# Two-layer transformer with a routed expert stage: whole rows scattered into the experts' lists in place of pairs

## The chip, the cores and the metric

The kernel runs on one core of one Trainium2 chip. The metric is the device time of one execution in microseconds; smaller is better. A core has TensorE (PE, matmuls), VectorE (DVE), ScalarE (ACT), GpSimd (POOL), SyncE (SP, which here only issues transfers) and 16 transfer engines, which serve the queue filled by SP and the queue filled by POOL.

## The reference, cut to what matters

Two layers work on 8 sequences of 512 tokens with 256 features, 4096 tokens in all. The change touches the last part of the second layer, `_L1_ffn_ref`: attention with 32 heads, then a second RMS norm, a router that gives each token its 4 best of 16 experts, and the experts' outputs summed with the router's weights.

```python
h = _rms(x, ff_ln_w)                       # x after the attention; (tokens, 256)
logits = h @ wg                            # 16 experts
topv, topi = jax.lax.top_k(logits, 4)
gate = jax.nn.softmax(topv, -1)
weights = zeros.at[..., topi].set(gate)
a = silu(einsum('bsd,edh->bseh', h, w1)) * einsum('bsd,edh->bseh', h, w3)
y = einsum('bseh,ehd->bsed', a, w2)
moe = einsum('bsed,bse->bsd', y, weights)
return x + moe
```

That result is multiplied by the layer's gate (`modr`, columns 1280 to 1535) and added to the layer's input. Everything is float32.

## The kernel before

The program is a row of phases, each with its own program per engine; `run` puts a fence between them (L197), at which every engine waits for all semaphores of the phase before. `phase_m` computes modulation rows, `phase_a` (about 30 to 1700 us) is the first attention, `phase_bc` the first expert layer and the second attention, `phase_d` (2527 to 4367 us) the third attention with the router, `phase_e` (4367 us to the end) the routed experts. Order within a phase is written out by hand: each engine runs its steps in program order and waits on semaphores. `Signal` keeps the counts (`mark` names a step, `at` gives its count), `chain` waits for the engine's own earlier results, `Ring` hands out PSUM banks.

In `phase_a` POOL has nothing but 64 small scatters into `list` (L1316 to L1319), one for every third group of exponentials, numbered c = 0 to 63.

In `phase_d` a batch is one sequence and has 64 steps (N = 64) of one head pair and one block of 128 queries. In each step TensorE makes scores, DVE takes their maxima (L2378), ACT the exponentials (L2207), DVE the reciprocal sums (L2387), POOL multiplies by these (`scale`, L2440), and TensorE transposes the result five or six steps later (`turn`, L2134). Between these, `before` pieces prepare the next batch by the table `ahead` (step 39, `h`: the normed rows for the projections, in the tile `h`) and `after` pieces finish the batch before by the table `late`: steps 14 and 15 `h2`, the second norm, into the same tile `h`; 16 `HT`, its transpose, and SP's write of the rows to `hrow` in HBM (L2026); 19 to 24 the router's logits, the four best (`top`, `topi`, as numbers `topf`), and the rank of each token in its expert's list, with `tally` the running lengths; 26 `gates`, which puts token number and weight as pairs into the tile `pair`; 27 `place`, which puts 4096 x expert + rank into `pos`; and from step 29 sixteen pieces `meta`, one a step, in each of which POOL scatters 128 pairs of 8 bytes to `meta` in HBM (L2413). At its start POOL fills `meta` with dummy entries, which point to 256 rows behind the tokens, and zeroes these rows and the two sums `acc0` and `acc1` of 4352 rows (L2444 to L2452), while SP loads the stage's inputs (L2008 to L2015), for all of which TensorE waits before its first projection.

`phase_e` first computes on DVE a table of 79 tiles (L2631 to L2650): a tile is 256 places of one expert's list; the table holds its first place (`ti[:, 0, t]`) and its expert (`ti[:, 1, t]`). SP loads X, the gates (L2511) and the table's constants ahead of it. Then for each tile t SP loads the 256 pairs (L2497; up to eight tiles ahead, when the add of tile t - 8 has landed) and the expert's weights of 768 KB (L2504, when the down product of tile t - 3 is done); POOL gathers 2 x 128 rows of `hrow` by the pairs (L2539); TensorE transposes them (L2565), multiplies by w1 and w3 (L2578) and by w2 (L2587); ACT and DVE do the activation; DVE multiplies by the weights in the pairs (L2667); and POOL adds the rows to one of the two sums with two accumulating scatters (L2548). The sums take turns: tile t adds to sum t % 2 once the add of tile t - 2 has landed, so that no two transfers in flight add to the same row. POOL's order is gather(t), add(t - 4). At the end SP loads both sums (L2523), and DVE adds them, multiplies by the gate and adds X (L2680 to L2686) in eight pieces, which SP stores (L2528).

Of the kernel before, what the change touches and what calls it, by code (L numbers as in the profile page):

```python
# [97 lines left out]
def consts():  # L98
    c = {}
# [53 lines left out]
    new = np.zeros((17 * 4096, 2), np.uint32)  # L153
    new[:, 0] = 4096 + np.arange(17 * 4096) % 256
    c["meta0"] = new
# [13 lines left out]
def program(nc, D, out):  # L169
    with ExitStack() as top:  # L170
# [261 lines left out]
        def phase_a(ctx, slots):  # L432
# [70 lines left out]
            tmp = sb("tmp", [128, 256])  # L503
            pe, dve, act, c_in = sig("a_tensor"), sig("a_vector"), sig("a_scalar"), sig("a_inputs")
# [801 lines left out]
            def pool(e):  # L1306
# [14 lines left out]
            return ((tensor, vector, scalar, pool, sync),  # L1321
                    (pe, dve, act, c_in, c_s, c_kv, c_kr, c_out, c_t, c_l, c_p, pool_, *c_x, *c_mb, *c_k6, *c_q6, *c_sel, *c_max),
# [547 lines left out]
        def phase_d(ctx, tally):  # L1870
# [19 lines left out]
            h = sb("h", [128, 4, 256])  # L1890
# [12 lines left out]
            tmp = sb("tmp", [128, 256])  # L1903
            zero = sb("zero", [128, 256])
# [11 lines left out]
            pair = sb("pair", [128, 2, 16, 2], U32)  # L1916
            pe, dve, act, pool_ = sig("d_tensor"), sig("d_vector"), sig("d_scalar"), sig("d_pool")
            c_l = sig("d_norm")
            c_in, c_h, c_n, c_x, c_o = sig("d_inputs"), sig("d_rows"), sig("d_new"), sig("d_x"), sig("d_out")
# [44 lines left out]
            late.update((29 + j, ("meta", j)) for j in range(16))  # L1964
# [34 lines left out]
            def sync(e):  # L1999
# [17 lines left out]
                def after(piece, k, b):  # L2017
# [6 lines left out]
                    elif piece == "HT":  # L2024
                        e.wait_ge(dve.sem, dve.at(("h2", b)))
                        e.dma_start(D["hrow"][512 * b:512 * b + 512, :].rearrange("(i p) d -> p i d", p=128), h[:]  # L2026
                                    ).then_inc(c_h.sem, c_h.mark(("h", b), 16))
# [201 lines left out]
            def vector(e):  # L2229
# [15 lines left out]
                def rms_rows(name, b, k, w):  # L2245
# [4 lines left out]
                    for i in (2 * k, 2 * k + 1):  # L2250
                        chain(e, dve)
                        e.scalar_tensor_tensor(h[:, i, :], y[:, i, :], rs[:, 2, i:i + 1], w, ALU.mult, ALU.mult
                                               ).then_inc(dve.sem, dve.mark((name, b)))

                def before(piece, k, b):
# [33 lines left out]
                def after(piece, k, b):  # L2289
# [5 lines left out]
                    elif piece == "h2":  # L2295
                        if k == 0 and b < 7:
                            e.wait_ge(pe.sem, pe.at(("hT", b + 1)))
                        rms_rows("h2", b, k, lnw[:, 1, :])
# [40 lines left out]
                    elif piece == "gates":  # L2339
                        if b >= 2:  # L2340
                            e.wait_ge(c_p[b % 2].sem, c_p[b % 2].at(("pair", b - 2)))
# [5 lines left out]
                        e.tensor_tensor(pair[:, b % 2, :, 1].bitcast(F32).rearrange("p (i k) -> p i k", k=4), ge[:],  # L2347
                                        gz[:, 1, :].unsqueeze(2).to_broadcast([128, 4, 4]), ALU.mult
                                        ).then_inc(dve.sem, dve.tick())
                        e.tensor_copy(pair[:, b % 2, :, 0].rearrange("p (i k) -> p i k", k=4),  # L2350
                                      tok[:, 4 * b:4 * b + 4].unsqueeze(2).to_broadcast([128, 4, 4])
                                      ).then_inc(dve.sem, dve.tick())
                    elif piece == "place":
# [7 lines left out]
                                      ).then_inc(dve.sem, dve.mark(("pos", b)))  # L2361

# [45 lines left out]
            def pool(e):  # L2408
                def after(piece, j, b):
                    if piece == "meta":  # L2410
                        if j == 0:
                            e.wait_ge(dve.sem, dve.at(("pos", b)))
                        e.indirect_dma_start(D["meta"], bass.IndirectOffsetOnAxis(pos[:, b % 2, j:j + 1], 0),  # L2413
                                             pair[:, b % 2, j, :], None
# [43 lines left out]
        def phase_e(ctx, tally):  # L2458
# [32 lines left out]
            def sync(e):  # L2491
# [22 lines left out]
                for t in range(T + 3):  # L2514
                    if t < T:
                        pairs(t)
# [274 lines left out]
```

## Time and profile before

| | us |
|---|---|
| median of three timed runs | 4997.76 (4989.64 to 5001.94) |
| span of the profiled execution, first to last instruction | 4945.7 |
| profiled execution, time besides the span | not given by the page |
| PE, DVE, ACT, POOL busy | 4241.6, 3176.8, 1929.8, 1642.4 |
| mean granted TensorE clock | 0.935 |

Busy time is that of the instructions themselves; a number in brackets behind a row of the timeline is the idle time of that engine ahead of it, and what ended it. Rows of POOL marked DMA_INDIRECT are the time in which POOL writes the transfer's descriptors, not the transfer. Landing is the time from issue to the semaphore.

### The profile page before, as it was taken

What the parts mean: (1) busy time and instruction counts of PE and PEld (TensorE: products, weight loads), DVE (VectorE), ACT (ScalarE), POOL (GpSimd) and SP (SyncE); (2) the same over time, 40 slices, a digit from 0 to 9 for tenths busy, and PEclk for the clock granted to TensorE, in tenths of its full rate; (3) what the DMA queues carried; (4) which work ended last, traced back from release to release, by engine and by line L of the source; (5) the groups of instructions that cost most, each with busy time, mean ns of one, the idle gap of its engine ahead of it and who ended that gap; (6) DMA issues with size and microseconds to landing.
All of it is one profiled execution on the core that took longest, in us unless ns stands there. A gap on an engine that the chain in (4) does not pass through costs nothing.

```text
span 4945.7 us, 68678 instructions
## 1 busy us (share of the span) xinstructions
PE 4241.6 (86%) x23426; PEld 2553.3 (52%) x23426; DVE 3176.8 (64%) x7341; ACT 1929.8 (39%) x4485; POOL 1642.4 (33%) x1384
## 2 busy tenths in 40 slices
PE   3698988888888895998858999999999999949985
PEld 1444544444454443775534555555555555547774
DVE  6788788878778775557635576666757666522223
ACT  0244435344443552322214455545555555511111
POOL 1000000000000002435004464546556554648885
PEclk6799999899999997999989999999999999979998
DMA  3211221211122106773041111111111111058888
GB/s 101 25 31 30 32 44 18 40 31 31 31 32 40 18 9 179 202 186 92 15 161 39 42 44 38 43 47 35 42 39 44 38 47 39 19 153 205 209 205 225
DMA packets 332115, 358.51 MB, mean 72 GB/s; under 512 B 177326, under 2 KB 257862, under 8 KB 330902
## 3 DMA queue, kind: packets, MB, share of 16 engines
q1 hardware_dynamic: 280888, 276.81, 21.6%
q0 software_dynamic: 47984, 76.34, 7.7%
q8 instruction: 190, 3.11, 0.3%
q14 instruction: 155, 1.27, 0.1%
q10 hardware_dynamic: 2898, 0.98, 0.1%
HBM read 212.35 MB, written 81.89 MB: 59 GB/s over the span
## 4 chain that ended last, share of the span: by engine, by line
PE 60%; DVE 22%; DMA 7%; ACT 4%; issue 3%; POOL 2%; SPq 1%; ACTq 0%; DVEq 0%; POOLq 0%
PE PS L2119 7%; DVE a_mm L1265 6%; PE PS L2104 6%; PE PS L2151 6%; PE PS L2134 5%; DMA e_xg<-hrow,e_mt 5%; PE PS L2161 4%; PE PS L914 3%; PE PS L854 2%; PE PS L1611 2%; PE PS L2122 2%; PE PS L881 2%; PE PS L719 2%; PE PS L2578 2%; PE PS L892 1%
## 5 line engine op out<-in xcount | busy, mean ns | idle before, releaser
L1265 DVE TENSOR_REDUCE a_mm<-PS 128x2 f32<-128x384 f32 (+4 forms) x1152 | 673.3, 610 | 232.6 <-PE PS L858 231.1
L2440 POOL TENSOR_TENSOR d_ef<-d_ef,d_zr 128x768 f32<-128x768 f32 (+3 forms) x512 | 640.1, 1258 | 449.9 <-DVE d_zr L2387 447.5
L1019 ACT ACTIVATE a_PT<-PS 128x512 f32<-128x512 f32 x896 | 514.9, 602 | 612.9 <-PE PS L892 397.0
L2207 ACT ACTIVATE d_ef<-PS,d_nm 128x128 f32<-128x128 f32 (+3 forms) x1024 | 529.3, 523 | 358.3 <-DVE d_zr L2387 298.6
L2378 DVE TENSOR_REDUCE d_nm<-PS 128x2 f32<-128x768 f32 (+3 forms) x512 | 419.3, 819 | 341.4 <-PE PS L2122 339.9
L1318 POOL DMA_INDIRECT list<-a_tok,slots x64 | 63.1, 986 | 1551.2 <-ACT a_PT L1019 1480.5
L2119 PE MATMUL PS<-d_k,d_q 64*128 64x128 f32 (+3 forms) x2048 | 421.3, 489 | 59.1 <-ACT d_ef L2207 41.2
L854 PE MATMUL PS<-a_K,a_Q 96*128 96x192 bf16 (+4 forms) x2048 | 420.0, 284 | 52.1 <-DVE a_mm L1265 22.9
L2134 PE MATMUL PS<-ident,d_ef 128*128 128x128 f32 x2560 | 369.2, 281 | 5.0 <-POOL d_ef L2440 4.1
L854 PEld LDWEIGHTS PS<-a_K,a_Q 80*128 80x128 bf16 (+1 forms) x2048 | 180.8, 103 | 357.3 <-DVE a_mm L1265 98.4
L2218 ACT ACTIVATE d_tf<-PS 128x512 f32<-128x512 f32 x320 | 190.7, 596 | 366.4 <-PE PS L2134 365.7
L881 PE MATMUL PS<-a_Q,a_K 83*128 83x512 bf16 (+1 forms) x704 | 273.1, 403 | 58.7 <-DVE a_mm L1265 35.2
L2119 PEld LDWEIGHTS PS<-d_k,d_q 64*128 64x128 f32 x2048 | 158.0, 189 | 293.9 <-issue 157.9
L2151 PE MATMUL PS<-d_tf,d_vt 128*64 128x512 f32 x1280 | 303.7, 604 | 3.9 <-ACT d_hT L2175 1.4
L2371 DVE TENSOR_TENSOR d_t<-PS,d_rope 128x1024 f32<-128x1024 f32 x160 | 195.2, 1224 | 168.0 <-PE PS L2104 153.7
L2134 PEld LDWEIGHTS PS<-ident,d_ef 128*128 128x128 f32 x2560 | 284.6, 146 | 6.8 <-issue 5.2
L2578 PE MATMUL PS<-e_xT,e_we 128*128 128x256 f32 x1264 | 287.1, 380 | 0.0
L2548 POOL DMA_INDIRECT acc<-e_ob,e_mt x158 | 252.1, 1596 | 60.8 <-issue 44.2
L2657 DVE TENSOR_TENSOR e_hm<-e_sg,PS 128x512 f32<-128x512 f32 x79 | 54.3, 688 | 317.9 <-PE PS L2578 289.9
L914 PE MATMUL PS<-a_PT,a_v 128*32 128x512 f32 (+1 forms) x2176 | 255.3, 559 | 3.5 <-ACT a_PT L1019 3.5
L2578 PEld LDWEIGHTS PS<-e_xT,e_we 128*128 128x128 f32 x1264 | 235.0, 191 | 28.9
L1482 POOL DMA_INDIRECT bc_big<-brow,bc_ids x126 | 119.7, 950 | 380.8 <-DMA brow<-bc_hb 241.1
(347 smaller groups left out, 8104.0 us busy)
## 6 DMA issues: line engine op xcount, KB each, us to landing
e_we<-in_exp SPq DMA_DIRECT2D x79, 768.0 KB, 5.4
d_q<-d_rr SPq DMA_DIRECT2D x512, 64.0 KB, 2.0
bc_big<-in_exp SPq DMA_DIRECT2D x63, 384.0 KB, 4.3
d_k<-d_rr SPq DMA_DIRECT2D x256, 64.0 KB, 2.0
yrow<-bc_ob SPq DMA_DIRECT2D x63, 256.0 KB, 4.6
a_Q<-scr SPq DMA_DIRECT2D x384, 32.0 KB
scr<-a_qsp SPq DMA_DIRECT2D x24, 384.0 KB, 3.0
acc<-d_zero POOLq DMA_DIRECT2D x2, 4352.0 KB, 37.6
```

What stands on the lines that cost most here:

```text
L854: e.matmul(p[:, n * k:n * k + n], Q6[0:rows, 4 * hh + g, qc], K6[0:rows, y, kind, hh, 128 * i + 128 - n:128 * i + 128], start=(k == 0), st ...
L881: mm_ = e.matmul(p[:, :], K6[0:rows, y, kind, hh, 128 * kt:128 * kt + 128], Q6[0:rows, 4 * hh:4 * hh + 4, 128 * i:128 * i + 128], start=Tr ...
L914: e.matmul(o, v, w, start=first, stop=last).then_inc(pe.sem, pe.mark(("pv", n)))
L1019: e.activation(PT[:, 4 * (n % 2) + q4, :], RS.of(("exp", n, q4))[:, :], ACT.Exp, scale=S0).then_inc(act.sem, act.mark(("exp", n, q4)))
L1265: e.tensor_reduce(mm[:, i % 2, kind, c:c + len(gs)], RP.of(("top", b, u, kind, gs[0]))[:, 0:len(gs) * n].rearrange("p (g k) -> p g k", g=l ...
L2119: e.matmul(p[:, r, 0:nk], q[rows, a % 2, hh, f, 128 * i:128 * i + 128], kd[rows, hp // 2, 2 * (hp % 2) + hh, 0:nk], start=True, stop=False)
L2134: e.transpose(p[:, 256 * f + 128 * r:256 * f + 128 * r + 128], ef[:, (2 * g + f) % 7, r, 128 * j:128 * j + 128], ident[:]).then_inc(pe.sem ...
L2151: e.matmul(p[64 * hh:64 * hh + 64, :], vt[:, b % 2, j, 64 * kv:64 * kv + 64], tf[:, place[2 * J + hh, j] % 12, :], start=(j == 0), stop=(j ...
L2207: e.activation(ef[:, n % 7, r, 0:nk], S.of(("exp", n))[:, r, 0:nk], ACT.Exp, bias=nm[:, n % 7, r:r + 1], accum_out=zz[:, n % 7, r:r + 1]). ...
L2378: e.tensor_reduce(nm[:, n % 7, :], S.of(("exp", n))[:, :, 0:128 * i + 128], AX, ALU.max, negate=True).then_inc(dve.sem, dve.mark(("max", n)))
L2440: e.tensor_tensor(ef[:, n % 7, :, 0:nk], ef[:, n % 7, :, 0:nk], zr[:, n % 7, :].unsqueeze(2).to_broadcast([128, 2, nk]), ALU.mult).then_in ...
L2578: e.matmul(p[:, 256 * m:256 * m + 256], we[:, t % 3, c0:c0 + 128], xT[:, t % 2, k, :], start=(k == 0), stop=(k == 1)).then_inc(pe.sem, pe. ...
```

## The change

Whole rows are scattered, not pairs. The tile `h` gets 9 more columns: the token number, the four weights, and the numbers of the four experts. POOL scatters each row of 265 numbers (1060 bytes) four times, to its place in each of its four experts' lists `xrow` in HBM, two scatters a step from step 28 in eight steps. The next use of the tile `h` (step 39, `h` of batch b + 2; for the last batch step 14) waits for these. The write to `hrow` is gone. The lists' first 256 rows and the sum are initialised by two transfers which POOL issues in `phase_a`, after its scatter c = 8; POOL's initial writes in `phase_d` are gone. The table is computed on DVE in `phase_d`, after the last batch's `place`, beside its scatters. A list's last tile is moved back so that it ends with the list, and rows which the tile before has already handled get the weight 0. `phase_e` loads a tile's 256 rows with one transfer from SP, takes the weight of its expert from the row's nine columns on DVE (`gates`), and adds into one sum; a tile's add waits until the add of the tile before has landed. X and the gates are loaded in eight parts during the tiles 8, 16, ... 64. The end has half of the sum's loads and two DVE operations per part in place of three.

```diff
@@ phase_a, pool
                     e.indirect_dma_start(D["list"], ...)
+                    if c == 8:
+                        e.dma_start(D["xrow"].rearrange("(e r) c -> e r c", r=4096)[:, 0:256, :],
+                                    D["row0"].unsqueeze(0).to_broadcast([17, 256, 265])).then_inc(c_n.sem, c_n.tick(16))
+                        e.dma_start(D["acc"], D["zero0"].to_broadcast([4352, 256])).then_inc(c_n.sem, c_n.tick(16))
@@ phase_d
-            late.update((29 + j, ("meta", j)) for j in range(16))
+            late.update((28 + j, ("meta", j)) for j in range(8))
@@ vector
                             if b >= 2:
                                 e.wait_ge(pe.sem, pe.at(("HT", b - 2)))
-                                e.wait_ge(c_h.sem, c_h.at(("h", b - 2)))
+                                e.wait_ge(c_p[b % 2].sem, c_p[b % 2].at(("row", b - 2)))
...
-                        e.tensor_tensor(pair[:, b % 2, :, 1]..., ge[:], gz[:, 1, :]..., ALU.mult)
-                        e.tensor_copy(pair[:, b % 2, :, 0]..., tok[:, 4 * b:4 * b + 4]...)
+                        e.tensor_tensor(h[:, :, 257:261], ge[:], gz[:, 1, :]..., ALU.mult)
+                        e.tensor_copy(h[:, :, 256:257].bitcast(U32), tok[:, 4 * b:4 * b + 4].unsqueeze(2))
+                        e.tensor_copy(h[:, :, 261:265], topf[:])
...
+                    elif piece == "meta" and k == 0 and b == 7:
+                        table()
@@ pool
-                        e.indirect_dma_start(D["meta"], bass.IndirectOffsetOnAxis(pos[:, b % 2, j:j + 1], 0),
-                                             pair[:, b % 2, j, :], None)
+                        for m in (2 * j, 2 * j + 1):
+                            e.indirect_dma_start(D["xrow"], bass.IndirectOffsetOnAxis(pos[:, b % 2, m:m + 1], 0),
+                                                 h[:, m // 4, :], None)
...
-                e.dma_start(D["meta"], D["meta0"])
-                e.dma_start(D["hrow"][4096:4352, :]..., zero[:]...)
-                for i in range(2):
-                    e.dma_start(D[f"acc{i}"]..., zero[:]...)
-                e.wait_ge(c_n.sem, c_n.at("new"))
@@ phase_e, sync
+                def rows(t):
+                    if t >= 4:
+                        e.wait_ge(pe.sem, pe.at(("xT", t - 4)))
+                        e.wait_ge(dve.sem, dve.at(("gates", t - 4)))
+                    row = e.value_load(ti[0:1, 0, t:t + 1], min_val=0, max_val=17 * 4096 - 256)
+                    e.dma_start(xg[:, t % 4, :, :].rearrange("p a c -> p (a c)"),
+                                D["xrow"][bass.ds(row, 256), :].rearrange("(p a) c -> p (a c)", a=2)
+                                ).then_inc(c_g[t % 4].sem, c_g[t % 4].mark(("rows", t), 16))
...
+                rows(0)
+                weights(0)
+                e.dma_start(place[:], D["place"])
+                for t in range(1, T + 1):
+                    if t < T:
+                        rows(t)
+                    if t >= 2:
+                        weights(t - 1)
+                    if t >= 8 and t % 8 == 0 and t < 72:
+                        later(t // 8 - 1)
@@ pool
-                for t in range(T + 4):
-                    if t < T:
-                        gather(t)
-                    if t >= 4:
-                        add(t - 4)
+                for t in range(T):
+                    e.wait_ge(dve.sem, dve.at(("out", t)))
+                    if t:
+                        e.wait_ge(c_a[(t - 1) % 2].sem, c_a[(t - 1) % 2].at(("add", t - 1)))
                     for a in range(2):
+                        e.indirect_dma_start(D["acc"], bass.IndirectOffsetOnAxis(to[:, t % 8, a:a + 1], 0),
+                                             ob[:, t % 4, a, :], None, compute_op=ALU.add
                                              ).then_inc(c_a[t % 2].sem, c_a[t % 2].mark(("add", t), 16))
@@ vector
+                def gates(t):
+                    if t >= 8:
+                        e.wait_ge(c_a[t % 2].sem, c_a[t % 2].at(("add", t - 8)))
+                    e.wait_ge(c_g[t % 4].sem, c_g[t % 4].at(("rows", t)))
+                    e.tensor_copy(to[:, t % 8, :].unsqueeze(2), xg[:, t % 4, :, 256:257].bitcast(U32))
+                    e.scalar_tensor_tensor(wt[:, t % 4, :, :], xg[:, t % 4, :, 261:265], tt[:, 0, t:t + 1],
+                                           xg[:, t % 4, :, 257:261], ALU.is_equal, ALU.mult)
+                    e.tensor_reduce(wr[:, t % 8, :], wt[:, t % 4, :, :], AX, ALU.add)
+                    e.scalar_tensor_tensor(wr[:, t % 8, :], place[:], tt[:, 1, t:t + 1], wr[:, t % 8, :], ALU.is_ge, ALU.mult)
...
                     if t < T:
                         gate(t)
+                    if t + 1 < T:
+                        gates(t + 1)
                     if t:
                         out(t - 1)
...
-                    e.tensor_tensor(ac[:, b, 0, :, :], ac[:, b, 0, :, :], ac[:, b, 1, :, :], ALU.add)
```

`table()` is the old table with one more product and sum over 80 x 16 elements and eight small operations; `later(b)` loads one eighth of X and one row of the gates.

## Rows read from the trace of the kernel before

**Rows 1.** Stage table: busy us per engine, clock, DMA share, GB/s.
```profile
core 0: us, PE busy (x) PEld busy (x) DVE busy (x) ACT busy (x) POOL busy (x), PEclk, DMA share, GB/s
4410.00:4902.00 492.00, 444.53 (x2153) 375.78 (x2151) 121.30 (x233) 90.75 (x152) 395.80 (x305) 1.00 0.85 203
4902.00:4945.70 43.70, 0.00 (x0) 0.00 (x0) 28.77 (x24) 0.00 (x0) 2.70 (x2) 0.51 0.90 297
```
**Rows 2.** Timeline of two adds and SP's pair load in the expert loop.
```profile
4595.37 1.62 POOL L2548 DMA_INDIRECT acc<-e_ob,e_mt  x1 [0.30 <-issue]
...
4597.30 1.56 POOL L2548 DMA_INDIRECT acc<-e_ob,e_mt  x1 [0.31 <-issue]
...
4601.86 0.34 SPq L2497 DMA_DIRECT2D e_mt<-meta  x1
```
**Rows 3.** POOL's indirect transfers by line: ns min/median/max, first and last start.
```profile
L2548 POOL DMA_INDIRECT acc<-e_ob,e_mt x158: 1554/1578/1638, 4410.0 to 4903.4; - x158
...
L2539 POOL DMA_INDIRECT e_xg<-hrow,e_mt x158: 942/972/1017, 4388.3 to 4881.8; - x158
...
L2413 POOL DMA_INDIRECT meta<-d_pair,d_pos x128: 954/1001/1068, 2913.8 to 4365.4; - x128
```
**Rows 4.** Chain of the expert loop: start, us, what.
```profile
4512.24 1.63 POOL acc L2548
4514.18 6.14 DMA acc<-e_ob,e_mt
...
4779.66 3.46 PE PS L2578 x16
...
4785.28 3.46 PE PS L2578 x16
```
**Rows 5.** Timeline from the last scatters to the first weight matmul.
```profile
4346.10 0.99 POOL L2413 DMA_INDIRECT meta<-d_pair,d_pos  x1 [29.51 <-DVE d_pos L2360]
...
4367.54 0.34 SPq L2507 DMA_DIRECT2D e_tab<-in_tiles  x1
...
4368.88 12.03 SPq L2511 DMA_DIRECT2D e_GB<-modr  x8
4370.37 0.18 DVE L2631 TENSOR_TENSOR e_cnt<-tally,e_tab 128x16 f32<-128x16 f32 x1 [24.54 <-DMA e_lte<-in_lte]
...
4379.05 0.20 DVE L2650 TENSOR_SCALAR e_ti<-e_tf 128x80 int32<-128x80 f32 x1
4381.72 3.66 SPq L2497 DMA_DIRECT2D e_mt<-meta  x4
...
4398.36 4.78 PE L2578 MATMUL PS<-e_xT,e_we 128*128 128x256 f32 x16
```
**Rows 6.** Timeline: SP's loads of the sums behind the last adds.
```profile
4907.14 17.64 SPq L2523 DMA_DIRECT2D e_ac<-acc  x16
```
**Rows 7.** Transfers from 2528 to 2570: all, and SP's queue.
```profile
DMA packets 4474, 16.40 MB, mean 391 GB/s; under 512 B 1040, under 2 KB 1552, under 8 KB 4074
...
q1 hardware_dynamic: 2400, 7.61, 47.3%
```
**Rows 8.** Timeline: the third attention's first projection and its operand.
```profile
2549.95 0.60 ACT L2175 ACTIVATE d_hT<-PS 128x512 f32<-128x512 f32 x1 [0.26 <-PE PS L2057]
...
2567.02 5.74 PE L2104 MATMUL PS<-d_hT,d_wk 128*128 128x512 f32 x8 [17.11 <-DMA d_tok<-in_tok]
```
**Rows 9.** Timeline of POOL in the first attention: the ninth list scatter.
```profile
404.03 0.96 POOL L1318 DMA_INDIRECT list<-a_tok,slots  x1 [13.22 <-ACT a_PT L1019]
```
**Rows 10.** Stage table of the 48 us behind it.
```profile
404.00:452.00 48.00, 39.44 (x283) 23.32 (x282) 41.88 (x129) 22.57 (x40) 1.91 (x2) 0.99 0.23 43
```
**Rows 11.** Timeline of a batch's scatters in the third attention, POOL and DVE.
```profile
2911.74 1.89 POOL L2440 TENSOR_TENSOR d_ef<-d_ef,d_zr 128x1024 f32<-128x1024 f32 x1 [1.73 <-DVE d_zr L2387]
...
2931.49 0.99 POOL L2413 DMA_INDIRECT meta<-d_pair,d_pos  x1 [0.16 <-issue]
...
2945.91 1.01 DVE L2252 SCALAR_TENSOR_TENSOR d_h<-d_y,rs,d_lnw 128x256 f32<-128x256 f32 x2
```
**Rows 12.** Page, issues: KB each, us to landing.
```profile
e_we<-in_exp SPq DMA_DIRECT2D x79, 768.0 KB, 5.4
```

More of the change, by code:

```diff
@@ L2023, in after @@
                         e.dma_start(xb[:], xout[:, 4 * b:4 * b + 4, :]).then_inc(c_x.sem, c_x.mark(("x2", b), 16))
[L2024 to L2027, printed above, removed]
+                        if b == 7:
+                            e.wait_ge(pe.sem, pe.at(("v", 7, 1, 1)))
+                            e.dma_start(tab, D["tiles"]).then_inc(c_b.sem, c_b.mark("table", 16))
+                            e.dma_start(lte, D["lte"]).then_inc(c_b.sem, c_b.mark("table", 16))
                     elif piece == "lg":
@@ L2361, in after, with reduced @@
                                       ).then_inc(dve.sem, dve.mark(("pos", b)))
+                    elif piece == "meta" and k == 0 and b == 7:
+                        table()
+                def reduced(out, a, b, op):
+                    n = out.shape[1]
+                    chain(e, dve)
+                    e.tensor_tensor(cmp[:, 0:n, :], a, b, op).then_inc(dve.sem, dve.tick())
+                    chain(e, dve)
+                    e.tensor_reduce(out, cmp[:, 0:n, :], AX, ALU.add).then_inc(dve.sem, dve.tick())
@@ L2481, in phase_e @@
             c_out = sig("e_out")
-            c_m = [sig(f"e_pairs{i}") for i in range(8)]
             c_w = [sig(f"e_weights{i}") for i in range(3)]
@@ L2505, in weights, with later @@
                                 ).then_inc(c_w[t % 3].sem, c_w[t % 3].mark(("weights", t), 16))
-                e.dma_start(tab[:], D["tiles"]).then_inc(c_in.sem, c_in.tick(16))
-                e.dma_start(lte[:], D["lte"]).then_inc(c_in.sem, c_in.mark("all", 16))
-                e.dma_start(Xs[:], xout).then_inc(c_x.sem, c_x.mark("x", 16))
-                for b in range(8):
+                def later(b):
+                    e.dma_start(Xs[:, 4 * b:4 * b + 4, :], xout[:, 4 * b:4 * b + 4, :]
+                                ).then_inc(c_x.sem, c_x.mark("x", 16))
                     e.dma_start(GB[:, b, :], D["modr"][b:b + 1, 1, 1280:1536].to_broadcast([128, 256])
                                 ).then_inc(c_gb.sem, c_gb.mark("all", 16))
-                e.wait_ge(dve.sem, dve.at("table"))
-                for t in range(T + 3):
+                rows(0)
+                weights(0)
+                e.dma_start(place[:], D["place"]).then_inc(c_in.sem, c_in.mark("all", 16))
+                for t in range(1, T + 1):
                     if t < T:
-                        pairs(t)
-                    if t >= 3:
-                        weights(t - 3)
+                        rows(t)
[3 more added lines that the diff above has]
+                        later(t // 8 - 1)
                 for i in range(2):
@@ L2646, in vector @@
-                e.tensor_scalar(tf[:, 2, :], tf[:, 0, :], 4096.0, None, ALU.mult).then_inc(dve.sem, dve.tick())
-                chain(e, dve)
-                e.scalar_tensor_tensor(ti[:, 0, :], tf[:, 1, :], 256.0, tf[:, 2, :], ALU.mult, ALU.add
-                                       ).then_inc(dve.sem, dve.tick())
-                e.tensor_scalar(ti[:, 1, :], tf[:, 0, :], 15.0, None, ALU.min).then_inc(dve.sem, dve.mark("table"))
+                    e.scalar_tensor_tensor(wr[:, t % 8, :], place[:], tt[:, 1, t:t + 1], wr[:, t % 8, :], ALU.is_ge,
+                                           ALU.mult).then_inc(dve.sem, dve.mark(("weight", t)))
@@ L2696, in program @@
         tally = sbt(top, "tally", [128, 16])
-        run(phase_d, tally)
-        run(phase_e, tally)
+        ti = sbt(top, "ti", [128, 2, 80], I32)
+        tt = sbt(top, "tt", [128, 2, 80])
+        run(phase_d, tally, ti, tt)
+        run(phase_e, ti, tt)
         for e in engines:
```

177 lines of the change are left out of this document (83 added, 94 removed).

## The prediction

> **What bounds the kernel now.** I read the stage table first, then the issue and line rows of the expert stage, then its chain and timeline. The page gives the profiled execution as a span, 4945.7 us, and no second time; the median of the three timed runs is 4997.76 us, so 52.1 us lie around the span. I make the sum on the span and add 52.1.
>
> In the stage table [rows 1] TensorE is near full only in the middle stages. From 4410 to 4902 (79 expert tiles) POOL is busy 395.8 of 492 us in 305 issues, and each issue has a 0.30 us gap before it [rows 2]: 395.8 + 305 x 0.30 = 487.3, so POOL is never free. That stage is bound by POOL's issuing: two gathers of 0.97 and two adds of 1.58 [rows 3], four gaps, 6.3 a tile. The adds begin at 4410.0 and the last of the 158 at 4903.4 [rows 3]; less one in-tile step of 1.93 [rows 2] that is (4903.4 - 4411.9)/78 = 6.30 us a tile. TensorE needs less: where its rows of the chain stand back to back, matmul block to matmul block is 4779.66 to 4785.28, 5.62 us [rows 4]. The granted clock is 1.00 there, the 2.4 GHz level, so TensorE has nothing more to give.
>
> **The expert loop: what takes the place of the gathers.** Both gathers and the pair load leave; SP loads 256 contiguous rows instead. POOL keeps two adds: 1.62 + 0.30 + 1.56 = 3.48 us. But there is now one sum, and every tile's adds wait until the tile before has landed (before: the tile before that one, which had two periods). So a period is issue plus landing plus wake-up. The landing has no row of its own; SP shows it. SP's pair load of 4601.86 waits for an add; the add before it was issued from 4595.37 and its second half ends at 4597.30 + 1.56 = 4598.86 [rows 2]: 3.0 us. Of this SP's own register work is about 0.76 (four such loads take 3.66 us, so 1.1 each, of which 0.34 is the issue [rows 5]). Landing plus wake-up: 2.24. The last adds give 4903.4 + 1.56 to SP's 4907.14: 2.1 to 2.2 [rows 3, 6]. A period is then 3.48 + 2.2 = 5.7, plus 0.1 for POOL's wake-up: 5.8.
> That is the undisturbed case. The disturbed one has a row: an add begun at 4512.24 is followed in the chain by 6.14 us of transfer from 4514.18, to 4520.32, 8.1 us after its start [rows 4]. Before, a second accumulator covered that; now it is paid. How often depends on load. The queues' engines are busy 0.85 of 6.30 us, 5.36 us a tile [rows 1]. The change swaps gathered for plain rows (about even) and spreads the loads of X and of the gates, once 5.2 MB at the stage's start, over the loop: at the tail's 297 GB/s with share 0.90 [rows 1] some 16 us, 0.2 a tile. So 5.56 of 5.8 us would be busy, 0.96: some adds must meet the weights' 768 KB. I take 6.1, one slow landing (8.1 + 0.3 against 5.8) in eight; ends 5.75 and 7.2 (half slow and the load on top). Loop: 78 x (6.10 - 6.30) = -16 us, between -43 and +70. A register load, two waits and a DMA stay on SP as before; DVE gets four small operations a tile, nearest the table's 0.18 [rows 5], under 0.8 us of a period in which DVE is busy 121 of 492 us [rows 1]. The first of them waits for the rows of tile t+1, and the output of tile t-1 is queued behind it; SP has issued those rows two tiles before TensorE turns them (it stops at the weights, which wait for the down product four tiles back), some 11 us against a landing of under 6, so this wait costs nothing, and 6 us and more if SP falls back.
>
> The Trainium skill (DMA: Bandwidth & Descriptors, Anatomy of one DMA) says a software-issued DMA costs about 2.0 us fixed, mostly the write's receipt, heaviest in HBM. It speaks against this edit, since a second sum hid that receipt. By it the 128 KB half lands 2.0 + 0.3 us after its issue, 5.8 a tile and -39 us for the loop; the undisturbed rows agree, the disturbed ones do not.
>
> **Start of the attention stage.** POOL's initial writes (two sums, pair table, dummy rows: by their shapes 9.7 MB) go. In 2528 to 2570 the engines move 16.40 MB at 391 GB/s [rows 7], while TensorE waits 17.11 us for the inputs until 2567.02; its other operand is there at 2549.95 + 0.60 [rows 8]. SP's queue has 7.61 MB of it [rows 7]; alone at that rate it takes 19.5 us, to about 2548, so the operand ends last. Gain 16.4 at most, 12 if SP's own issuing of the last inputs stays slow; I take 15.5. What is late next is that operand (DVE's norms).
> These writes, now 9.1 MB, are issued in the first attention behind the ninth list scatter, at 404.03 [rows 9]. There DMA share is 0.23, TensorE and DVE busy 39 and 42 of 48 us [rows 10]. By the rate above they land in 23 to 40 us, and SP's small loads meet them. Nobody waits for them but the stage's end, 1290 us on. Loads are early by a tile; cost 2 us, between 0 and 15. The list scatters behind them are also only awaited at the end.
>
> **Scatters of whole rows.** 128 issues stay 128. A pair scatter takes 1.00 us, a gather of 1 KB rows 0.97, an accumulating issue 1.58 [rows 3]; the width did not matter between the first two, so I take 1.00 for 1060-byte rows, ends 0.95 and 1.6. They are now two a step in eight steps. For the first such batch POOL begins with the scaling of 2911.74, and the seventh scatter stands at 2931.49 [rows 11]. Nine more by then at 1.17 are 10.5 us, of which its gaps absorb 2 or 3: the last is issued near 2940 and lands some 3 us on, as the adds do, near 2943. DVE's next use of the tile, which now waits for that, is at 2945.91. The three us cover it; behind that wait on DVE stand the maxima that every exponential needs, so uncovered it would cost. POOL's scalings come up to 5 us late, within the five steps until TensorE transposes them. I take +1, ends 0 and +47 (rival below). The row write on SP and its wait go, at nothing: no chain piece held them.
> The last batch still has 16 issues from 4346.10; the last starts at 4365.4 [rows 3, 5], and SP proceeded at 4367.54. A 135 KB landing is longer than 1 KB's: +1.2.
>
> **Start of the expert stage.** The table took 4370.37 to 4379.25 on DVE [rows 5]. Now it runs from 4346 beside the scatters, with two 1.49 us operations and a few small more: 13 us, 8 us of cover. Uncovered it would cost 13. SP's eight gate loads (12.03 us), X, and the gathers' wait for pairs go from the head. Before: 4367.5 to the first weight matmul 4398.36, 30.9 us [rows 5]. After, from the same point: register load 0.8; rows(0); weights(0) issued at 1.9, landing 5.4 later [rows 12], 7.3; rows(1) behind it, about 8; transposes 1.2: 9.3. Gain 21.6, less the 1.2 above: 20.4 (ends 15 and 23).
>
> **Tail.** Before, 12.6 MB of loads and stores and 24 DVE operations, 28.77 us [rows 1]; without the second sum 8.4 MB and 16 operations, 19.2. Gain by DVE 9.6; by bytes 4.2 MB at the stage's 297/0.90 = 330 GB/s, 12.7. The smaller decides, with the pair of first loads now one: I take 10, ends 8 and 13.
>
> **Sum.** -16 - 15.5 + 2 + 1 - 20.4 - 10 = -58.9; span 4886.8, time **4939**.
>
> **Rivals.**
> 1. *TensorE becomes the bound*: every add lands undisturbed. For it: two landings of 2.2. Against: engines 0.96 busy. Period 5.75: 78 x 0.35 = 27 less, 4912. Chance 0.2.
> 2. *The landing of the single sum takes the place of the gathers, the other side*: adds and the weights' transfer share the engines in most tiles. For it: the 8.1 us row. Against: only two adds are queued at a time now, and SP's loads wait for TensorE, which follows the adds, so the two may fall apart. At 7.2 a tile, 78 x 1.1 = 86 more, 5025, slower. It decides from 6.1 + 58.9/78 = 6.85. Chance 0.14. The Trainium skill (DMA: Bandwidth & Descriptors, Queues, rings and completion order) says that an engine alternates between queues packet by packet; that would be this mechanism.
> 3. *A 1060-byte scatter costs an accumulating issue's 1.58*: 16 x 0.58 = 9.3 us a batch; DVE's wait uncovered by 6 in six batches, 37, and 9.3 in the last: +46, 4985. Against: width was free from 8 bytes to 1 KB. Chance 0.11.
> 4. *The engines are simply full*: unaligned rows cost more than gathers, period 6.5: +31, 4970. Chance 0.1.
> The forecast, period 5.9 to 6.4, 4920 to 4965: 0.45.
>
> **How the numbers follow.** About 0.3% (15 us) is what a measurement of this kernel can tell. Faster by more: 0.45 + 0.2 + 0.08 + 0.04 = 0.77 (most of 4, part of 3); within: 0.1; slower: 0.13. Leaving out rival 2 and a little at both ends gives 4900 to 4998.
>
> **What would show it.** Period of the adds 6.1; POOL's idle time before them given to the add's own transfer, not to "issue"; first weight matmul 9 to 10 us after SP's first load; first attention matmul near 2551; 34 us from the last tile's first add to the end; scatters of 1.0 us. Wrong if the adds' period is over 6.85, or if DVE waits for scatters in the attention.

## The result, and the profile after

The changed kernel takes 5163.59 us (5156.55 to 5168.56, four runs), the kernel before 4997.91 beside it: ratio 1.0333, 95% interval 1.0319 to 1.0347. Forecast were 4939 and a range of 4900 to 4998. The change makes the kernel slower by 3.3%.

Two sizes must be kept apart first. In the profile of after the time is 5168.56 and the span 5166.8, so only 1.8 us lie around a span. The 52.1 us that the prediction put there go with the chip: the kernel before took 4998 us in the runs beside this one and in one later set of runs, 4949, 4956 and 4950 in the three others. Its profile (4945.7) has the time of the second kind of chip, the profile of after that of the first. (Each chip served for one set of runs, so what is called the chip's here could also be the occasion's.) The table therefore sets the changed kernel's second profile (run `e7_changed_again`, on a chip of the second kind) against before; each column is a distance between first or last rows of the traces.

| stretch | before | changed (e7) | difference | forecast |
|---|---|---|---|---|
| start to last list scatter | 1691.1 | 1834.9 | +143.8 | +2 |
| the middle stage (first experts, second attention), to the third attention's first transpose | 856.9 | 857.5 | +0.6 | 0 |
| to the first projection | 19.0 | 2.7 | -16.3 | -15.5 |
| to the last scatter of rows or pairs | 1798.4 | 1807.4 | +9.0 | +1 |
| to the first add | 44.6 | 24.2 | -20.4 | -20.4 |
| 78 periods of the adds (from one tile's first add to the next one's) | 491.5 | 556.5 | +65.0 | -16 |
| tail | 44.2 | 32.5 | -11.7 | -10 |
| span | 4945.7 | 5115.7 | +170.0 | -58.9 |

Two rows went wrong, the first attention and the expert loop; together they are 223 us off. All rows that follow are of the first profile of after, if nothing else is said. The first attention behind the ninth list scatter, by stretches (columns as in [rows 1]):

```profile
404.00:452.00 48.00, 21.75 (x119) 12.40 (x116) 19.38 (x43) 8.69 (x16) 5.04 (x4) 0.68 0.78 84
452.00:500.00 48.00, 26.24 (x164) 15.31 (x164) 27.14 (x93) 14.34 (x24) 0.99 (x1) 0.71 0.43 64
500.00:550.00 50.00, 0.00 (x0) 0.00 (x0) 0.00 (x0) 0.00 (x0) 0.00 (x0) 0.50 0.06 27
550.00:600.00 50.00, 3.96 (x19) 1.21 (x19) 0.00 (x0) 0.60 (x1) 0.00 (x0) 0.53 0.13 41
```

The first row answers to [rows 10], where TensorE was busy 39.44 us. In the third row no engine does anything for 50 us, and the transfer engines are busy 0.06 of the time: one sixteenth. Bandwidth is not what is short; one of the sixteen is at work. Who waits is shown by SP's queue and by the waits (us in total, times, longest):

```profile
463.22 129.39 SPq L671 DMA_DIRECT2D a_Q<-scr  x11
```
```profile
PE PS L856 <- DMA a_Q<-a_selT: 98.9, 1, 98.9
```

SP's eleven small loads take 129 us to issue, and TensorE stands 98.9 us in one wait for the load before them. Behind both is one of the two initial writes (KB, us to landing):

```profile
xrow<-in_row POOLq DMA_DIRECT2D x1, 4505.0 KB, 58.4
acc<-in_zero POOLq DMA_DIRECT2D x1, 4352.0 KB, 186.2
```

The two count on one semaphore, so the landings may be exchanged. The records of single packets tell them apart: from 407.3 to 580.5 there are 85 packets of 54,272 bytes, 2.0 us each (the first 3.4), none beside another. 85 x 54,272 bytes are the 17 x 256 dummy rows.

The third attention and the expert stage (min/median/max ns, first and last start), answering to [rows 3]; the rows of the kernel's first projection and weight matmul, to [rows 8] and [rows 5]:

```profile
L2467 POOL DMA_INDIRECT xrow<-d_h,d_pos x128: 956/991/1481, 3095.4 to 4561.3; - x128
...
L2581 POOL DMA_INDIRECT acc<-e_ob,e_to x158: 1550/1557/1616, 4585.5 to 5135.9; - x158
```
```profile
2752.04 5.88 PE L2113 MATMUL PS<-d_hT,d_wk 128*128 128x512 f32 x8 [1.20 <-DMA d_tok<-in_tok]
...
4573.46 4.76 PE L2605 MATMUL PS<-e_xT,e_we 128*128 128x256 f32 x16
```

A scatter of 1060-byte rows costs POOL 0.99 us as one of 8 bytes did. The wait before the first projection is 1.20 us, not 17.11, and the first weight matmul stands 12.2 us behind the last scatter. The adds have (5135.9 - 1.86 - 4585.5)/78 = 7.03 us a tile, before 6.30. The loop's and the tail's row of the stage table:

```profile
4585.50:5134.00 548.50, 460.75 (x2151) 384.12 (x2149) 163.88 (x537) 90.74 (x152) 242.91 (x156) 0.95 0.78 193
5134.00:5166.80 32.80, 0.00 (x0) 0.00 (x0) 18.98 (x16) 0.00 (x0) 3.11 (x2) 0.50 0.85 264
```

POOL, 395.8 of 492 us before, is now busy 242.9 of 548.5: it is no longer full, and the loop is slower all the same. The chain of waits says why. An undisturbed period and a slow one (start, us, what):

```profile
4700.89 3.73 DMA acc<-e_ob,e_to
...
4705.35 1.56 POOL acc L2581
4706.90 0.30 issue
4707.21 3.82 DMA acc<-e_ob,e_to
...
4711.76 1.56 POOL acc L2581
```
```profile
4803.36 5.96 DMA acc<-e_ob,e_to
...
4810.23 0.55 issue
4810.78 1.56 POOL acc L2581
```

Undisturbed: 1.86 from the first half's issue to the second's, 3.73 to 3.82 until that has landed, and 0.74 until POOL begins the next add: 6.3 to 6.4. The outputs between the landing and the add belong to a later tile: DVE's four buffers are full, since POOL is some four tiles behind. POOL does not wait for them: in the first seven periods, where these outputs start 2.7 to 17 us behind the landing, POOL begins 0.73 us after it as well. In the slow period the same landing takes 5.96. Slow periods are the smaller part: of the 78, 51 are under 6.6 us and 15 over 7.6, these 9.2 in the mean.

Last, a mark of the first kind of chip, in the chain of the middle stage; two of five such pieces:

```profile
2413.11 7.04 another core or an unknown queue
...
2420.93 10.43 another core or an unknown queue
```

The five make 33.7 us. The profiles of e7 and of before have none.

### The profile page after: what moved, and what is told of

The parts are those of the page before. It is cut to its first block, busy times and chain, and to the rows that moved or that the text cites. A ratio compares the mean times of both kernels' runs of the same rounds, so it can differ in the third digit from the quotient of the medians.

```text
span 5166.8 us, 68882 instructions
## 1 busy us (share of the span) xinstructions
PE 4278.3 (83%) x23426; PEld 2569.6 (50%) x23426; DVE 3225.2 (62%) x7665; ACT 1929.1 (37%) x4485; POOL 1478.2 (29%) x1223
## 4 chain that ended last, share of the span: by engine, by line
PE 54%; DVE 23%; DMA 8%; SPq 4%; issue 4%; ACT 4%; POOL 3%; another core or an unknown queue 1%; ACTq 0%; DVEq 0%; POOLq 0%
PE PS L2128 6%; PE PS L2113 6%; DMA acc<-e_ob,e_to 6%; DVE a_mm L1267 5%; PE PS L2160 5%; PE PS L2143 5%; PE PS L2170 3%; PE PS L916 3%; SPq L671 3%; PE PS L856 2%; POOL acc L2581 2%; PE PS L1617 2%; PE PS L2131 2%; PE PS L883 2%; PE PS L721 2%
## 5 line engine op out<-in xcount | busy, mean ns | idle before, releaser
L2581 POOL DMA_INDIRECT acc<-e_ob,e_to x158 | 246.0, 1557 | 329.2 <-DVE e_ob L2681 273.9
L2681 DVE TENSOR_SCALAR e_ob<-PS,e_wr 128x256 f32<-128x256 f32 x158 | 69.2, 480 | 315.6 <-DMA acc<-e_ob,e_to 299.3
L2480 POOL TENSOR_TENSOR d_rr<-d_t 128x512 f32<-128x512 f32 x80 | 101.6, 1270 | 560.4 <-DVE d_t L2424 445.6
```

## The experiments

All ratios are to the kernel before on the same chip, with the 95% interval.

**e1_rows_spread.** One transfer engine against bytes.

```diff
-  e.dma_start(D["xrow"].rearrange("(e r) c -> e r c", r=4096)[:, 0:256, :],
-              D["row0"].unsqueeze(0).to_broadcast([17, 256, 265]))
+  e.dma_start(D["xrow"].rearrange("(e r) c -> r e c", r=4096)[0:256, :, :],
+              D["row0"].unsqueeze(1).to_broadcast([256, 17, 265]))
```

> The changed kernel with one edit: the DMA that writes the 17 x 256 dummy rows runs over rows first and lists second (256 x 17 x 1060 bytes instead of 17 runs of 271 KB); bytes, place and number of DMAs stay. Theory (one transfer engine): the trace of the changed kernel has this DMA as 85 packets of 54,272 bytes, one behind the other at 2.01 us, from 407.3 to 580.5, and the small loads of the first attention wait behind them; that is the 150 us by which the first attention is longer. Then this kernel wins nearly all of it: the last list scatter near 1695 (before 1691, changed 1841), the time 5163.6 - 145 = about 5018, and the wait of TensorE from 500 to 590 gone. Rival (bytes, or the zero fill of the sum in 4 KB packets): 9.1 MB are still written at this place, so 80 us and more of the 150 stay, time over 5090. The expert loop stays at 7.0 us a tile under both.

Measured 5017.03 us, ratio 1.0148 (1.0126 to 1.0169). The time meets the 5018 only because this chip is 50 us faster: the ratio fell by 0.0185, some 92 us. The last list scatter is at 1745.1, not 1695: 90 to 96 us come back, 54 stay. Order of the dimensions alone is worth 90 us; but the rival had a part of the truth. The trace has the rest (stage table of e1):

```profile
450.00:500.00 50.00, 8.60 (x45) 3.64 (x43) 9.25 (x28) 5.65 (x8) 0.99 (x1) 0.58 0.95 71
```

All sixteen engines are busy, 0.95, at 71 GB/s: something else is slow. By the packet records it is the zero fill: its 1088 packets of 4 KB take 949 ns each (median), those of the fill of the kernel before 164 ns. The latter reads a tile of zeroes in SBUF, the former one 1 KB row of DRAM again and again. That both ends lie in DRAM does not explain it: the dummy rows' 1088 packets of 4,240 bytes, DRAM to DRAM too but from 256 different rows, take 316 ns in the same run.

**e2_two_sums.** On e1, two sums, one zero fill more, and a tail that reads and adds both.

```diff
-  if t: e.wait_ge(c_a[(t - 1) % 2].sem, c_a[(t - 1) % 2].at(("add", t - 1)))
+  if t >= 2: e.wait_ge(c_a[t % 2].sem, c_a[t % 2].at(("add", t - 2)))
-  e.indirect_dma_start(D["acc"], ...)
+  e.indirect_dma_start(D[f"acc{t % 2}"], ...)
```

> The kernel of the run before it (dummy rows spread) with two sums again: tile t adds into sum t mod 2 and waits for tile t - 2, both sums are zeroed in the first attention, and the tail reads and adds both. Theory (the single sum's landing bounds the loop: issue start 1.86 after issue start, 1.56 of issue, 2.2 to land, 0.7 for POOL to go on, 6.3 undisturbed and 7 to 9 where the landing is slow): the adds' period falls from 7.03 to TensorE's 5.6 to 5.9 us a tile, 78 x 1.2 = -94, the tail is 10 longer: 84 under the run before it, near 4935. Rival (the engines' load by whole rows and weights, 5.5 us a tile of packet time, and DVE's order bound the loop): the period stays over 6.6 and the time over 4990.

Measured 5011.99, ratio 1.0131 (1.0110 to 1.0151). The period came as expected, the total did not: the second fill from the DRAM row put the last list scatter at 1818.3, 73 us later, and ate the gain.

```profile
L2584 POOL DMA_INDIRECT acc<-e_ob,e_to x158: 1556/1562/1613, 4506.9 to 4969.4; - x158
```

(4969.4 - 1.86 - 4506.9)/78 = 5.91 us a tile, more than half of the periods 5.62, TensorE's own. With two sums the loop is fast, so the single sum is what makes it slow. Whole rows and DVE's four small operations are in this run too.

**e3_before_one_sum.** The kernel before, all tiles into `acc0`, waiting for tile t - 1; one fill and one half of the tail's work less.

> The kernel before with one sum alone: every tile adds into the same sum and waits for the tile before; one zero fill, one half of the tail's loads and additions less. Theory (the landing chain is the bound): POOL's two gathers (2.5 us with gaps) fit in the 2.9 us in which it waits for the landing, so the period is the chain's 6.3 to 7.1, not 6.3 as before: loop 0 to +60, tail -10, the attention's start -10: time between 4980 and 5050, POOL's idle time before the first add of a pair given to the add's transfer or to an output that waits for it. Rival (whole rows and not the single sum make the loop slow): period 6.3 to 6.4, POOL still full, time 4975 to 4985.

Measured 5037.49, ratio 1.0189 (1.0166 to 1.0211), within the expected time, but the period is 7.67, longer than expected. POOL in that loop:

```profile
4703.35 1.56 POOL L2548 DMA_INDIRECT acc<-e_ob,e_mt  x1 [0.30 <-PE PS L2578]
4705.22 1.01 POOL L2539 DMA_INDIRECT e_xg<-hrow,e_mt  x1 [0.30 <-issue]
4706.53 0.97 POOL L2539 DMA_INDIRECT e_xg<-hrow,e_mt  x1 [0.30 <-issue]
4709.12 1.63 POOL L2548 DMA_INDIRECT acc<-e_ob,e_mt  x1 [1.61 <-DVE e_ob L2667]
```

The gathers do fit into the wait, but the next add begins 5.77 us after the second half's issue, not 4.5. The landing is what is later: 5.0 us in the median, in the changed kernel 3.8. That the gathers' transfers, issued in between on the same queue, cause this is likely, but not shown apart. One sum alone costs 78 x 1.37 = 107 us there; the changed kernel, with one sum and no gathers, stands at 7.03 to 7.13.

**e4_half_weights.** On e1; SP returns for odd t, and tile t uses the weights of tile t - t % 2.

> The kernel of the first run (dummy rows spread, one sum) with the weights loaded for every second tile only; the odd tiles compute with the weights of the tile before. It leaves out 39 of 79 loads of 768 KB. Theory (a slow landing is an add whose packets meet the weights' transfer): landings of over 4.5 us get rare, the adds' period falls from 7.03 to 6.3 to 6.45, the chain's own length, and no lower. Rival 1 (the landing is slow by itself, for instance by the adds' own reads and writes): period stays at 6.9 to 7.1. Rival 2 (TensorE or the load of the engines is the bound): period under 6.0.

Measured 5005.49 us in one run; period 6.83. None of the three: with half the loads gone the period is 0.16 under e1's 6.99, of the 0.6 that lie over the undisturbed one. Four profiles with the same loop (after, e7, e1, e5) have 7.03, 7.13, 6.99 and 7.13, so 0.16 is hardly more than their spread.

**e5_zero_tile.** On e1, the single sum zeroed from SBUF.

```diff
-  e.dma_start(D["acc"], D["zero0"].to_broadcast([4352, 256]))
+  e.dma_start(D["acc"].rearrange("(i p) d -> p i d", p=128),
+              z0[:].unsqueeze(1).to_broadcast([128, 34, 256]))
```

> The changed kernel with spread dummy rows and, new, the sum zeroed from a tile of zeroes in SBUF (128 partitions, as the kernel before did it in its last attention) instead of from one 1 KB row of DRAM. With spread rows alone the first attention was still 54 us longer than before, and the 1088 packets of 4 KB took 949 ns each there, against 164 ns in the attention stage of the kernel before. Theory (a DRAM row that every packet reads is a slow source, 16 engines in the same place): the packets take about 170 ns, the fill 12 us instead of 65, the last list scatter stands 5 to 15 us behind before's 1691, and the time is 5017 - 43 = about 4975. Rival (small loads suffer from any 4.4 MB put at this place, whatever its source): less than 15 us come back, time over 5000.

Measured 4979.56, ratio 1.0056 (1.0039 to 1.0072). The packets take 164 ns, the last list scatter is at 1697.4. In the stretch that answers to the row of e1 above TensorE works, and the engines have room:

```profile
450.00:500.00 50.00, 39.83 (x199) 19.65 (x197) 42.46 (x100) 15.40 (x27) 1.57 (x2) 0.86 0.17 45
```

With the source, the order in which the fill writes its rows changed too, so the two are not shown apart. The 143.8 us of the first attention are therefore 90 for the dummy rows' form, 48 for the zeroes' source (with its order) and 6 that are left. In the seven traces with both mended the last list scatter starts between 1695.2 and 1705.5, so the 6 are not well resolved.

**e6_zero_tile_two_sums.** e5 with e2's two sums, both zeroed from SBUF.

> Spread rows, both sums zeroed from the SBUF tile, two sums in the expert loop. Theory: the two-sum loop at 5.9 us a tile and the cheap start of the first attention add up: 5012 - (127 - 20) = about 4905, 40 us under the kernel before on this chip (4946 by its profiled span). Rival (the first attention keeps most of its loss): over 4950.

Measured 4900.57, ratio 0.9897 (0.9881 to 0.9914): faster than before by 1%. Period 5.89.

**e8_pieces_two_sums**, and **e8_again**. On e6, the writes in 17 x 3 pieces.

```diff
-  if c == 8:     # all initial writes at once
+  if 8 <= c < 25:
+      k = c - 8  # 256 dummy rows of list k, rows 256k to 256k + 255 of both sums
```

> As the run before it (two sums, SBUF zeroes), but the initial writes cut into 17 x 3 pieces of 256 and 265 KB, three behind each list scatter from the ninth to the twenty-fifth. Theory (what costs is that small loads queue behind megabytes on every transfer engine): a piece is gone in about 2 us, so no load waits long, and the last list scatter falls to within 5 us of before's 1691; time 5 to 15 under the run before it. Rival (the bytes cost in any form, or POOL's 51 issues of about 1 us delay the list scatters' chain): the same time or more.

> The kernel with cut initial writes and two sums once more, as the partner of the next run on the same chip. Expected: the same ratio to before, 0.988 within 0.002.

Measured 4893.26, ratio 0.9876 (0.9859 to 0.9892), and again 4894.99, 0.9884 (0.9864 to 0.9904). Against e6 that is inside the intervals, and the last list scatter (1705.5, 1696.9; e6 1699.9) shows no gain: with a good form and source it hardly matters whether the writes go at once or in pieces. The repeated run came as expected.

**e7_changed_again.** The changed kernel, unedited, on this chip.

> The changed kernel, nothing edited, on this chip. In its own profile the middle stage (first experts and second attention) was about 50 us longer than before, with stretches between two TensorE instructions that name no releaser; the kernel before was also 52 us slower in its timed runs there (4998) than in its profile (4946). Theory (that belongs to the chip it ran on, and to both kernels): here the middle stage takes before's 857 us, the time is about 5165 - 52 = 5113, and the ratio to before stays 1.033. Rival (it is the change's own, the instruction stream): the stage stays 50 us long and the ratio is 1.043.

Measured 5118.02, ratio 1.0335 (1.0317 to 1.0352); middle stage 857.5. The 50 us go with the chip, in both kernels; run e11 met such a chip again (before 4998.01, its own middle stage 10 + 43 us longer).

**e9_last_scatters_apart.** On e8.

```diff
-  for m in (2 * j, 2 * j + 1):
+  for m in ((j,) if b == 6 else (2 * j, 2 * j + 1) if j < 8 else ()):
```

> The kernel of the run before it, with the 16 row scatters of the seventh batch spread over 16 steps of the last batch's attention, one a step, instead of two a step over eight. Theory (in the last batch no projections of a next one fill TensorE, and POOL's scalings come late behind two scatters a step: 1.9 + 2 x 1.29 = 4.5 us of POOL for a step of 3.4; the trace has TensorE waiting 2.6 us for a scaling at that place, and the stage from the first projection to the last scatter is 1807 instead of before's 1798): 3 to 6 us come back, the last batch's product of gates and rows starts 152 to 154 us after the one before it instead of 157. Rival (the 8 us are the lower clock of TensorE at the end and longer small operations of DVE): no change within 2 us.

Measured 4888.69, ratio 0.9876 (0.9858 to 0.9895), beside e8_again's 0.9884: the times do not resolve it. The two traces differ as expected: from first projection to last scatter 1801.4 instead of 1806.7, and between the last two batches' transposes of rows 152.8 instead of 157.3 (before 152.4). The wait it removes, in e7:

```profile
4366.87 1.79 PE L2143 MATMUL PS<-ident,d_ef 128*128 128x128 f32 x8 [2.59 <-POOL d_ef L2494]
```

This is the lowest time of the study, 61 us under before.

**e10_no_weights.** On e5, SP's `weights` returns for t >= 3, and tile t uses the weights of tile t % 3.

> The changed kernel with spread rows, SBUF zeroes and one sum, and the weights loaded for the first three tiles only; all other tiles compute with these. It leaves out 76 of 79 loads of 768 KB. With half of the loads the period fell only from 6.99 to 6.83. Theory (the slow landings, 7 to 10 us a period, are adds whose second half is queued behind a 768 KB load that SP issued between the two halves; with half the loads the others met more often): the period falls to the chain's own 6.4 to 6.5, with slow ones left only where X and the gates are loaded, every eighth tile. Rival (the adds are slow by themselves or by the row loads): it stays over 6.7.

Measured 4957.31 in one run. Period 6.88: 0.25 less than e5's, but over the 6.7 from which the rival was to be right. The weights are a part, not the cause.

**e11_rows_only.** On e10, `later(b)` for all b ahead of `rows(0)`, so that in the loop SP loads rows alone.

> The kernel of the run before (one sum, weights loaded for three tiles only, the rest of the tiles with these) and the loads of X and of the gates all at the head of the expert stage: in the loop SP loads nothing but the rows, 265 KB a tile. Theory (each load that SP puts between an add's issue and its landing makes it late; the last eight tiles of the run before, with no load left, take 6.2 to 6.4): the periods of 8 to 9.5 us at every eighth tile go, the mean falls from 6.88 to 6.7, and what stays over 6.25 is the row loads'. Rival (every eighth tile is slow by its data, for instance by its tokens): they stay. The head of the stage takes about 15 us longer under both.

Measured 5015.78 in one run, on a chip where before took 4998.01. Period 6.73, and no period over 7.61 is left, where e10 had five of 8.2 to 9.4. The three rows of adds (e5, e10, e11, in this order):

```profile
L2586 POOL DMA_INDIRECT acc<-e_ob,e_to x158: 1550/1557/1612, 4386.0 to 4944.1; - x158
```
```profile
L2586 POOL DMA_INDIRECT acc<-e_ob,e_to x158: 1551/1558/1615, 4386.3 to 4924.5; - x158
```
```profile
L2586 POOL DMA_INDIRECT acc<-e_ob,e_to x158: 1551/1557/1612, 4456.4 to 4983.1; - x158
```

7.13, 6.88, 6.73. The last eight periods of e11, when SP has nothing more to load, are 6.17 to 6.49, in the mean 6.30: the chain by itself. From e5's 7.13 the mean falls by 0.25 without the weights, by 0.15 more without X and the gates, and 0.43 are left over 6.30 in e11. These are steps in this order, not the shares of the three in e5, and the first two are near the spread of 0.14. The single periods show it:

| | under 6.6 us | over 7.6 us | median |
|---|---|---|---|
| after | 51 | 15 | 6.42 |
| e5 | 48 | 19 | 6.52 |
| e10 | 19 | 5 | 6.72 |
| e11 | 23 | 1 (7.61) | 6.73 |

Without the weights the long periods go, and the usual one gets longer: SP now issues the rows elsewhere, in most of e11's periods 1.85 us after the add's start, with its second half, where after has them some 5.0 us behind it. What the row loads cost in the changed kernel itself no run shows. What is shown is that the long periods come with the weights and with X and the gates.

What a late landing looks like is seen packet by packet in the slow period of after. The packets that start in each microsecond:

```
us        adds (1 KB)   rows (2120 B)   weights (6 KB)
4804      90            24               1
4805      62             1               0
4806      81             0              22
4807       1             0              47
4808       2            27              44
4809       0            79              14
```

SP issues the weights at 4805.12, between the issue of the add's second half (4803.36) and its landing. 253 of the add's 256 packets have started by 4806.9. The last three start at 4807.19, 4808.35 and 4808.68, among the weights' packets, and the landing is reported at 4809.32. Three late packets of 256 make the landing 2.1 us longer, and POOL's wake-up behind it is 1.46 here. But a load in that place does not always do this. In the undisturbed period above, where the add started at 4705.35 and landed in time, SP issued its weights just as late:

```profile
4708.96 0.34 SPq L2546 DMA_DIRECT2D e_we<-in_exp  x1
```

In 70 of after's 78 periods the weights are issued between the second half and its landing; 44 of these are under 6.6 us and 15 over 7.6. Of the other eight none is over 7.6. So every slow landing there had a load beside it, most landings with one were not slow, and what decides which adds are hit is open.

## Why the prediction was wrong

**First attention, +2 (0 to 15) against +144: the step that failed most.** It priced 9.1 MB "by the rate above", 391 GB/s of [rows 7], the rate of loads and of fills from SBUF, of other shapes. It did not hold: the dummy rows ran on one engine (27 GB/s), and the zeroes came from a single DRAM row (4 KB in 949 ns in e1). In place of 23 to 40 us the dummy rows alone took 173. The sentence that nobody waits for the writes but the stage's end was true and beside the point, since SP's small loads share the engines; that they "are early by a tile" was no cover against one engine taken for 173 us. What was left once form and source were mended, 6 us, lies in the range that was given. The Trainium skill (DMA: Bandwidth & Descriptors, Why a DMA increments its semaphore by 16 and not by 1) says that a transfer uses the largest number of engines up to 16 that divides the slowest dimension (other than 1) of both sides, which for 17 is one and for 256 and 4352 sixteen. For some copies issued by GpSimd it names an exception, which this one did not show. The rule could have been read against the diff before the run, and the trace agrees: 85 packets, none beside another, and a landing after 31.7 us once 256 stood first (e1).

**Expert loop, 6.10 against 7.03 to 7.13: mis-sized in two terms.** The mechanism was named: issue plus landing plus wake-up, lengthened by slow landings. The chain by itself was set at 5.8 and is 6.30 to 6.4. Issue (3.42 for 3.48) and landing (2.2 for 2.2) held; POOL's wake-up was put at 0.1 and is 0.74. That term is 50 us. The value had no row behind it, and the trace of before had one that spoke against it. POOL was never free in the loop, but ahead of it it waited for the pairs to land:

```profile
4381.72 5.77 DMA e_mt<-meta
...
4387.55 0.73 issue
4388.28 0.99 POOL e_xg L2539
```

Its first gather starts 0.79 us after that landing at 4387.49. The disturbances were put at 0.3 a tile, one period in eight at 8.4 us; they are 0.7 to 0.8, in after 15 of 78 periods, one in five, at 9.2. Rival 2 (the single sum's landing, the other side) named the direction, and its deciding period of 6.85 was passed, but only in part by its own mechanism: adds and weights meet in time in most tiles (70 of 78), yet most periods stay undisturbed (51 of 78), and the wake-up makes up the rest. It was given 0.14, on the argument that adds and loads "may fall apart"; SP's loads are released by TensorE, which follows the adds, and in these 70 periods that puts them beside each other instead.

**The third attention, +1 against +9.** The scatter's price (1.00) was right, rival 3 fell (0.99), and DVE's wait for the scatters stayed covered: batch follows batch every 218.8 us (e7), before every 218.0. POOL's late scalings were taken as harmless everywhere; in the last batch, with no projections of a next one to fill TensorE, they cost 5 (e9 against e8_again, one trace each). The other 4 were not tried; 0.8 us a batch over six batches would be of that size.

**Right:** start of the attention stage (-16.3 for -15.5), start of the expert stage (-20.4 for -20.4), tail (-11.7 for -10), DVE's four operations and the tile table hidden. These three gains, 48 us, stand in every run of the changed kernel with one sum, but for e11, where X and the gates are loaded at the head of the expert stage; with two sums the tail's goes.

**The 52.1 us** were taken as something around the span; around a span lie 1.8 us. They go with the chip, and why such a chip is slower in the middle stage stays open.

## What to carry to other kernels

Price an initial write by its own shape and source, and look at who shares the engines with it, even if no one waits for it. When two buffers that take turns are made one, the full round trip, issue, landing and the issuer's wake-up, becomes the period, and a load that falls between issue and landing can lengthen it. An engine that is full in one stage shows its wake-up in another: look for a place where it waits for a landing, here its first gather, before putting a number to such a term. And periods of one loop should be looked at one by one: their mean fell from e5 to e10 while the usual period rose.

## What the runs showed of the hardware

- A POOL transfer of 17 runs of 271 KB went as 85 packets in a row, 2.0 us each, DMA share 0.06; the same bytes as 256 x 17 rows landed in 31.7 us (e1). Eleven small loads of SP's queue took 129 us to issue beside it.
- 4 KB packets whose source is one 1 KB DRAM row: 949 ns (e1), in after 786; from an SBUF tile: 164 ns (before, e5). Packets of 4,240 bytes from 256 different DRAM rows: 316 ns (e1).
- POOL went on 0.73 us after an add's landing in 76 of after's 78 periods, and 1.46 us in two; in before 0.79 us after the pairs' landing.
- Three late packets of 256 made a landing 5.96 us instead of 3.8 (after).
- The kernel before ran at 4998 us on two chips and at 4950 on three others. The profiles of after and e11 have the difference in the middle stage, as TensorE idle time that no row of this core ends.
